# Stacked gate features and 64-column gate products in a cross-attention layer on Trainium2

## The reference

```python
emb = box_relational_embedding(boxes)      # [b, n, m, 16]: sin and cos of
                                           # 100 * log-distance (x, y) and 100 * log-size (w, h)
g = relu(einsum('bnmd,hd->bhnm', emb, Wg) + bg)
a = einsum('bhqd,bhkd->bhqk', q, k) / sqrt(64)
mn = softmax(log(clip(g, 1e-6)) + a, axis=-1)
out = einsum('bhqk,bhkd->bqhd', mn, v) @ Wo.T + bo
```

## Time and profile before

| | |
|---|---|
| Time, three runs | 1159.33, 1161.57, 1162.9 us; median 1161.57 us |
| The profiled execution | 1160.38 us, with a span of 1158.5 us |
| Mean granted clock of TensorE | 0.925 of full speed |
| PE, DVE, ACT, POOL busy | 83%, 71%, 59%, 62% of the span |
| First attention | from the start to about 476 us |
| Period of one box in its steady part | 23.7 us |

### The profile page before, as it was taken

One profiled execution on the slowest core, in us unless ns is written; L12 is line 12 of the kernel. 1 busy time (PEld: TensorE's weight loads), 2 busy tenths in 40 slices (PEclk: granted clock), 3 DMA queues, 4 the chain that ended last, 5 costly groups with the idle time before them and its releaser, 6 DMA issues.

```text
span 1158.5 us, 32871 instructions
## 1 busy us (share of the span) xinstructions
PE 958.8 (83%) x12178; PEld 778.2 (67%) x12178; DVE 822.9 (71%) x1947; ACT 683.9 (59%) x1338; POOL 712.6 (62%) x811
## 2 busy tenths in 40 slices
PE   0549999999999974679878469993899999999996
PEld 0346777777777753445554358871799999999995
DVE  3988887788778867468777689966566566666663
ACT  2457888888888863065426368864354444444452
POOL 2988888876776672034512569974566666666672
PEclk9878999999999997589989679985899999999998
DMA  9276776787677755500001000002553225832251
GB/s 285 66 197 138 137 143 157 161 194 151 153 155 143 135 121 137 187 7 1 1 26 44 5 2 21 21 21 92 170 156 94 32 45 166 259 88 32 31 143 14
DMA packets 52117, 119.65 MB, mean 103 GB/s; under 512 B 7616, under 2 KB 30144, under 8 KB 51632
## 3 DMA queue, kind: packets, MB, share of 16 engines
q0 software_dynamic: 14144, 35.48, 21.3%
q1 hardware_dynamic: 35520, 80.71, 20.5%
q10 hardware_dynamic: 2352, 2.10, 0.6%
HBM read 212.54 MB, written 37.85 MB: 216 GB/s over the span
## 4 chain that ended last, share of the span: by engine, by line
PE 51%; DVE 17%; POOL 11%; ACT 9%; issue 6%; DMA 4%; ACTq 0%; SPq 0%; POOLq 0%; DVEq 0%
PE bank L2107 17%; PE bank L2121 9%; POOL PT L560 5%; PE bank L1786 5%; PE bank L1689 3%; ACT EX L1393 2%; PE bank L1728 2%; PE bank L1766 2%; DVE h L1063 2%; DVE nmx L1177 2%; PE bank L1937 2%; ACT L1362 1%; PE bank L1721 1%; PE bank L1899 1%; ACT fks L1362 1%
## 5 line engine op out<-in xcount | busy, mean ns | idle before, releaser
L1623 ACT ACTIVATE yg<-bank,bms 128x128 f32<-128x128 f32 x312 | 105.7, 363 | 113.1 <-PE bank L2107 106.0
L1296 DVE TENSOR_TENSOR hm<-hf,hm 128x256 f16<-128x256 f32 x156 | 66.8, 428 | 99.7 <-ACT hm L1630 94.2
L2107 PE MATMUL bank<-xT,wm_even 128*128 128x128 f16 x1920 | 117.7, 221 | 3.1 <-DVE hf L1291 1.8
L1291 DVE SCALAR_TENSOR_TENSOR hf<-bank,bms,yg 128x128 f32<-128x128 f32 x312 | 98.6, 346 | 26.9 <-ACT yg L1623 25.8
L707 POOL DMA_INDIRECT out_x<-ys,sidx x39 | 62.7, 1608 | 86.2 <-DVE ys L1310 86.2
L2107 PEld LDWEIGHTS bank<-xT,wm_even 128*128 128x128 f16 x1920 | 111.5, 99 | 6.2 <-DVE hf L1291 3.9
L2107 PE MATMUL bank<-xT,wm_odd 128*128 128x128 f16 x1824 | 110.1, 219 | 2.3 <-DVE hf L1291 2.3
L2107 PEld LDWEIGHTS bank<-xT,wm_odd 128*128 128x128 f16 x1824 | 104.2, 98 | 4.9 <-DVE hf L1291 2.4
L1630 ACT ACTIVATE hm<-hf 128x256 f16<-128x256 f32 x156 | 64.6, 414 | 69.0 <-DVE hf L1291 68.2
L560 POOL TENSOR_TENSOR PT<-PT 128x512 f16<-128x512 f32 x64 | 72.3, 1158 | 42.7 <-ACT PT L1419 42.7
L619 POOL TENSOR_TENSOR h<-h 128x512 f16<-128x512 f32 x32 | 40.6, 1281 | 81.8 <-DVE h L1063 79.8
(11 more groups left out here) (308 smaller groups left out, 2658.7 us busy)
## 6 DMA issues: line engine op xcount, KB each, us to landing
wm_even<-expert_weights SPq DMA_DIRECT2D x60, 1024.0 KB
wm_odd<-expert_weights SPq DMA_DIRECT2D x57, 1024.0 KB
expert_weights<-in_wcat POOLq DMA_DIRECT2D x16, 768.0 KB, 8.0
wsp<-expert_weights SPq DMA_DIRECT2D x16, 768.0 KB, 4.3
wsp<-in_wcat POOLq DMA_DIRECT2D x16, 768.0 KB, 10.8
expert_weights<-wsp SPq DMA_DIRECT2D x16, 768.0 KB, 3.3
Lst<-gate_tables SPq DMA_DIRECT2D x48, 68.0 KB, 5.9
gate_tables<-Lw SPq DMA_DIRECT2D x6, 512.0 KB, 4.6
```

Of the source, the lines that this page charges most:

```text
L1291: v.scalar_tensor_tensor(hf[:, (c // 2) % 2, c % 2, :], bank[c % 4][:, MT:2 * MT], bms[:, par, FC + c:FC + c + 1], yg[:, c % 4, :], ALU.ad ...
L1296: v.tensor_tensor(hm16[:, par, 1, c - 1:c + 1, :], hf[:, q % 2, :, :], hm16[:, par, 0, c - 1:c + 1, :], ALU.subtract).then_inc(m_hl, 1)
L1623: s.activation(yg[:, c % 4, :], bank[c % 4][:, 0:MT], ACT.Gelu, bias=bms[:, par, c:c + 1]).then_inc(m_g, 1)
L2107: ins = t.matmul(bank[c % 4][:, w * MT:(w + 1) * MT], wm16[par][:, wp, col:col + P], xT16[:, par, xp * KD + kk, :], start=(n == 0), stop=( ...
```

## The change

The feature tile is laid out anew: its rows are now four groups (q) of 32, each with 4 queries times 8 features. For each box, transfers on the chip build `Fst`, 96 rows by 4 groups by 1024 columns: rows 0 to 31 and 32 to 63 hold the high part of group q, rows 64 to 95 its low part. The weights become a tile of 96 rows by 64 columns (16 heads x 4 queries): high, low, high. One product over 96 rows then sums all three pairs, and a gate of two j takes eight products of 64 columns (two j times four q) where it took six of 256. The result goes to the same bank, in steps of 4 out of 16 columns.

`F16s` now has one buffer and so has `Fst`. New on SP are `stack_high(b)`, 8 transfers of 64 KB, behind `s_fhi` and the gates of box b-1, and `stack_low(b)`, 4 transfers of 64 KB, behind `s_flo`. They stand: `stack_high(0)` ahead of `store_tables(0)`, `stack_low(0)` behind the first table loads; those of box b-1 in the place of box b, behind `load_tables(b)` and ahead of `store_half` and `load_half`; those of box 15 ahead of the last but one `store_half`. PE's gate 0, ACT's fp16 copy and POOL's `feature_low` wait for all stacks of their box or of the box before. The loads of box coordinates are now two of 1 MB (four of 512 KB before), and `We` is smaller. DVE's reciprocal (L882) counts on another semaphore.

```diff
+QN = 4
+QR = 2 * QN * 4
+FR = 3 * QR
+STK = 16 * 3 * (NN // QN)
-        F16s = sb("F16s", [P, 2, 2, NJ * N], F16, l0)
+        F16s = sb("F16s", [P, 2, NJ * N], F16, l0)
+        Fst = sb("Fst", [P, NN // QN, NJ * N], F16, l0)
...
+            def stack_high(b):
+
+                sp.wait_ge(s_fhi, b + 1)
+                if b:
+                    sp.wait_ge(s_gf, 4 * b)
+                for q in range(NN // QN):
+                    for k in range(2):
+                        sp.dma_start(Fst[k * QR:k * QR + QR, q, :], F16s[q * QR:q * QR + QR, 0, :]).then_inc(s_fst, 16)
+
+            def stack_low(b):
+
+                sp.wait_ge(s_flo, b + 1)
+                for q in range(NN // QN):
+                    sp.dma_start(Fst[2 * QR:3 * QR, q, :], F16s[q * QR:q * QR + QR, 1, :]).then_inc(s_fst, 16)
+
             for par in range(2):
                 next_ctx(par, par)
+            stack_high(0)
             store_tables(0)
             for par in range(2):
                 load_tables(par)
+            stack_low(0)
             for par in range(2):
                 load_half(0, par, True)
...
+            for b in range(2, B):
+                par = b % 2
+                if b < B - 2:
+                    next_ctx(b, par)
+                if b == NJ:
+                    store_tables(1)
+                load_tables(b)
+                stack_high(b - 1)
+                stack_low(b - 1)
+                store_half(b // 2 - 1, par)
+                load_half(b // 2, par)
+
+            stack_high(B - 1)
+            stack_low(B - 1)
             store_half(E - 1, 0)
             sp.wait_ge(s_qf, 6 * B)
...
             def feature_low(n, par):
                 gp.wait_ge(s_fhi, n + 1)
-                nc.gpsimd.tensor_tensor(F16s[:, par, 1, :], fs, F16s[:, par, 0, :], ALU.subtract).then_inc(s_flo, 1)
+                if n:
+                    gp.wait_ge(s_fst, STK * n)
+                nc.gpsimd.tensor_tensor(F16s[:, 1, :], fs, F16s[:, 0, :], ALU.subtract).then_inc(s_flo, 1)
...
-                if first > 1:
-                    ac.wait_ge(s_gf, 4 * n - 4)
-                s.activation(F16s[:, par, 0, :], fs, ACT.Copy).then_inc(s_fhi, 1)
+                if n:
+                    ac.wait_ge(s_fst, STK * n)
+                s.activation(F16s[:, 0, :], fs, ACT.Copy).then_inc(s_fhi, 1)
...
                 if g == 0:
-                    pe.wait_ge(s_flo, b + 1)
+                    pe.wait_ge(s_fst, STK * (b + 1))
...
-                    for n, (wp, fp) in enumerate(PAIRS):
-                        ins = t.matmul(bk[:, jj * 256:(jj + 1) * 256], F16s[:, par, fp, j * N:(j + 1) * N], We16[:, wp, :], start=False,
-                                       stop=(n == 2), skip_group_check=True)
+                    part = bk[:, jj * 256:(jj + 1) * 256].rearrange("p (h q i) -> p q h i", h=H, q=NN // QN)
+                    for q in range(NN // QN):
+                        ins = t.matmul(part[:, q, :, :], Fst[0:FR, q, j * N:(j + 1) * N], We16[0:FR, :], start=False, stop=True,
+                                       skip_group_check=True)
```

More of the change, by code:

```diff
@@ L122, in build @@
         R16 = sb("R16", [P, 2, 2, N], F16, l0)
-        We = sb("We", [P, H * NN], F32, l0)
-        We16 = sb("We16", [P, 2, H * NN], F16, l0)
+        We = sb("We", [P, H * QN], F32, l0)
+        We16 = sb("We16", [P, H * QN], F16, l0)
         WoT = sb("WoT", [P, CH, D], F32, l0)
@@ L339, in _ @@
             sp.dma_start(AB[:, :, :], a["AB"]).then_inc(s_cs, 16)
-            sp.dma_start(We[:, :], a["We"]).then_inc(s_cs, 16)
+            sp.dma_start(We[0:FR, :], a["We"]).then_inc(s_cs, 16)
             for j in range(3):
@@ L346, in _ @@
             sp.dma_start(boxn[:, :, :], a["boxn"]).then_inc(s_cw, 16)
-            for xy in range(2):
-                for e in range(2):
-                    sp.dma_start((cm, rows)[e][64 * xy:64 * xy + 64, :], a["boxm"][xy, e, :].partition_broadcast(64)).then_inc(s_cw, 16)
+            for e in range(2):
+                sp.dma_start((cm, rows)[e][:, :], a["boxm"][e]).then_inc(s_cw, 16)
             sp.dma_start(bqk[:, :, :], a["bqk"]).then_inc(s_o, 16)
@@ L881, in take_pv @@
                         dv.wait_ge(s_oe, 4 * c + f - 1)
-                    v.reciprocal(rden[:, f % 2, :].unsqueeze(2), ps[:, :, DK:DK + 1]).then_inc(s_rd, 1)
-                    dv.wait_ge(s_rd, 4 * c + f + 1)
+                    step(v.reciprocal(rden[:, f % 2, :].unsqueeze(2), ps[:, :, DK:DK + 1]))
                     if f == 0 and not first:
@@ L932, in _ @@
             xn_low(1, 1)
-            dv.wait_ge(s_cw, 16 * 5)
+            dv.wait_ge(s_cw, 16 * 3)
             step(v.tensor_tensor(cn[:, :], boxn[:, :, 0], boxn[:, :, 1], ALU.add))
@@ L2157, in arrange @@
     bn = lohi.transpose(4, 2, 0, 1, 3)
-    a["boxn"] = c(np.broadcast_to(bn[:, None], (2, 4, NN, B, NJ, 2)).reshape(P, B * NJ, 2))
-    a["boxm"] = c(boxes.reshape(T, 2, 2).transpose(2, 1, 0))
+    bn = bn.reshape(2, NN // QN, QN, B, NJ, 2).transpose(1, 0, 2, 3, 4, 5)
+    a["boxn"] = c(np.broadcast_to(bn[:, :, None], (NN // QN, 2, 4, QN, B, NJ, 2)).reshape(P, B * NJ, 2))
+    bm = boxes.reshape(T, 2, 2).transpose(1, 2, 0)
+    a["boxm"] = c(np.broadcast_to(bm[:, None, :, None], (2, NN // QN, 2, 4 * QN, T)).reshape(2, P, T))
     delta = np.array([(s >> 1) & 1 if s < 8 else 0 for s in range(SLOTS)])
@@ L2165, in arrange @@
     feat = lambda sc, dl, fr: Wg[:, sc * 8 + dl * 2 + fr]
-    We = np.zeros((2, 2, 2, NN, H, NN), np.float32)
+    We = np.zeros((3, 2, 2, 2, QN, H, QN), np.float32)
     for xy in range(2):
@@ L2169, in arrange @@
             for fr in range(2):
-                for nn in range(NN):
-                    We[xy, sc, fr, nn, :, nn] = feat(sc, xy, fr)
-    a["We"] = We.reshape(P, H * NN)
+                for i in range(QN):
+                    We[:, xy, sc, fr, i, :, i] = feat(sc, xy, fr)
+    a["We"] = We.reshape(FR, H * QN)
     AB = np.zeros((SLOTS, 2, H), np.float32)
@@ L2183, in arrange @@
     for p in range(P):
-        sc, fr = (p >> 5) & 1, (p >> 4) & 1
+        sc, fr = (p >> 3) & 1, (p >> 2) & 1
         cst[p, 0], cst[p, 1] = turn[fr], 0.25 * sc
```

9 lines of the change are left out of this document (5 added, 4 removed).

## The result

The changed kernel takes 1181.38 us (median of 4 runs, 1178.33 to 1182.59) beside 1160.45 for the kernel before: ratio 1.0176, 95% interval 1.0146 to 1.0206. It is slower, as predicted, but by 21 us and not by 8 to 9; the time lies above the range, which ended at 1179.0. The profiled execution took 1178.33 us with a span of 1176.5, 18.0 us more than before.

The account below looks back on a forecast made before the run. A 23.7 us chain of waits through ACT, POOL and PE, without the gate products, was taken as the bound; 0.8 + 2.4 + 5.0 = +8.2 us on 1160.38 gave 1168.6, plus 1.2 for the median: 1169.8 us, range 1164.0 to 1179.0.

Parts of the forecast that it names:

- What bounds the kernel: Steady box of the first attention: a 23.7 us chain of waits without the gate products bounds it, not PE's work.
- that sign of being right: Steady box: PE's idle time ahead of the value products at about 1.4 us, with the period still 23.7.
- Part 1: Gate products on PE: a gate falls from 1.08 to 0.68 us, a box by 1.6 us; term 0.
- Part 2: Stacks in a steady box: complete by 229.1 us at the median landing, gate 0 at 230.98; term 0.
- Late stacks in every box: Rival, slower: twelve stacks land 9.2 us after the last issue, delaying every gate 0; 1180 us, chance 0.10.
- Part 3: Box 7: its stacks, queued behind the second tables, delay gate 0; +2.4 us, bounds +1.0 and +7.2.
- Part 4: Feed-forward weights: box 15's stacks ahead of these loads on SP delay DVE; +5.0 us, bounds +4.2 and +8.1.
- Part 5: First box: stacks and tables fall among POOL's conversions, less a shorter gate; +0.8 us, bounds -0.5 and +2.5.
- gates on the path: Rival, faster: PE is the limit, so 1.6 us of each box come off; 1144 us, chance 0.06.
- cheap issues: Rival, no change: SP issues a small stack transfer in 0.05 us, not 0.42; 1164 us, chance 0.11.
- dear products: Rival, slower: a small gate product costs the same 127 ns as one of 256 columns; 1177 us, chance 0.04.
- the ring: 23.7 us chain per box: exponentials, ACT, POOL's low parts, PE's value products to scores, next exponentials; gate products outside it.

Follow-up runs that it names:

- b1: Kernel before the change, with one of three pairs of feature products in the gates (two products instead of six), no stacks; 1160.35 us, ratio 1.0013.
- b2: Changed kernel with 128 unused products on PE ahead of gate 0 of box 7, filling its wait; 1176.98 us, ratio 1.0183 to the kernel before.
- a2: Changed kernel with the high stack of box 0 issued behind the first table stores, ahead of the wait for their landing; 1176.84 us, ratio 1.0141.
- a3: Changed kernel with the low stack of box 15 issued behind the four feed-forward weight loads instead of ahead; 1177.18 us, ratio 1.0148.
- a1: Changed kernel with both stacks of box 7 issued ahead of the second set of tables; 1181.61 us, ratio 1.0184 to the kernel before.
- b3: Changed kernel with POOL's two converting transfers of expert weights held back until the first tables have landed; 1167.41 us, one run, no ratio.
- e1: Kernel before, early feed-forward loads, stacks moved in their best order and waited for ahead of gate 0 but never read; 1157.96 us, ratio 1.0046.
- e2: Same as e1 but PE does not wait for the stacks, which are moved and never read; 1155.90 us, ratio 1.0026 to the kernel before.
- c1: Changed kernel with box 7's stacks issued between the second set of table stores and SP's wait for their landing; 1171.48 us, ratio 1.0126.

## Why the prediction was right or wrong

**What bounds the kernel: right.** Neither the ordinary periods of after nor those of b1 moved, and the idle time grew where the prediction put it ahead of the second half of the scores (0.62 us for 0.6). The larger part appeared ahead of the row scores (1.39 us), where PE waits for DVE, and not ahead of the value products (0.25 us, as before, for a forecast 1.45): that sign of being right did not come.

**Part 1, gate products: right.** 43 ns for a forecast 45; a gate takes 0.65 us for 0.68. The Trainium skill ("TensorE: Matmul & The Clock Gate", section "LDWEIGHTS (loading the stationary operand)") gives 107 ns for each weight load by its formula; as a pitch of products with a load each, the trace of after disagrees as that of before did.

**Part 2, ordinary boxes: right, with margin.** Less the 4.0 us of the first box the low stack of after starts at 221.9, as predicted, and with a median landing of 2.0 us (in ordinary boxes at most 2.7) it is there 4 to 6 us before gate 0. The DMA share rose to 0.85 where 0.82 was predicted. Late stacks in every box did not occur.

**Part 3, box 7: the mechanism right, three sizes wrong.** With 4.0 us taken off, the table loads start at 248.5, as they did. From there: (1) "twelve issues at 0.42 us" took 7.76 us in place of 5.0. The price came from a table load of 16 rows, and a stack transfer of 32 rows takes 0.59 us and a gap of 0.04 (that the rows make the difference is not shown). The last issue starts 2.6 us later than I had it. (2) The landing was 5.35 us, not 3.5: +1.85. I chose the value near the local row, but POOL's conversion was already in flight, which I had named and priced at 1.3 us. (3) The clock was left out, although the first box showed a granted 0.50 behind a stretch without products: a wait of 7 us halves it, and b2 prices that at 2.8 us. With 2.4 predicted, 2.6 and 1.85 explain a lateness of 6.85 us, and b2, whose clock stays up, measures 6.6. With the half clock this is the 9.4 us seen. My upper bound of +7.2 had the longest landing but neither the issue price nor the clock. So the steps that failed are the price of an issue, the landing, and a clock term put at nothing without a reason. The last is also the least certain size: a2 and a3 have 1.7 and 4.0 us for it. The text also had both parts of the stack ready "long before" the table loads; a1 shows the low part only 2 to 3 us ahead of them, which is why a1's move failed.

**Part 4, feed-forward weights: right.** +4.65 for +5.0. The four low issues took 2.41 us in place of 1.7, and the last landing was 0.7 us shorter than before (8.80, 9.52). The lower bound of +4.2 has no working: the four issues alone gave +4.4. The 0.6 us that came back behind it was not foreseen.

**Part 5, the first box: wrong, +4.0 for +0.8.** The step that failed is the one that costs the push by volume ("0.26 MB ... at 2.9 us for 1 MB"). Volume did not matter. What mattered is that the eight issues of high stacks, 5.06 us, moved the tables behind POOL's conversions on the DMA engines, and that SP stands for the tables' landing. I had these stacks and the conversions in one sentence and did not follow the wait `s_ts` that lies between them; a2 and b3 each undo it in their own way. The 0.5 us that a shorter gate was to give back are not shown: the next period is 1.5 us shorter, but in e1 and e2, with the gates of before, as well.

**The sum.** The forecast was 1169.8 us and the measured time is 1181.4. Of this miss 9.8 us are the terms: 3.2 in the first box, 7.0 in box 7, and -0.4 in the rest. The other 1.9 us are that the median of after lies 3.1 us above its profiled execution where that of before, of three runs, lay 1.2. What they are is not shown: executions in which one more stack is late (e1) or in which the lower clock lasts longer (a3) would fit. Of the rivals, late stacks have come true in one place only; gates on the path, cheap issues and dear products are ruled out.

## What to carry to other kernels

Where one queue both issues and waits, price what a new transfer pushes behind the queue's next wait, and which other queue's long transfer it is now behind: here eight cheap issues made a landing 7 us longer and the first box 4.0 us later, and moving them a few lines gave 3.6 of these back. Small transfers belong in the time that the queue stands anyway. Check that the engine that a change relieves is in the ring at all; a kernel with part of its work left out tells that in one run.

## What the runs showed of the hardware that was not expected

- The issue of a 64 KB stack transfer, between two tiles in on-chip memory, takes SP 0.59 us and a gap of 0.04 in after, beside 0.42 with the gap for the table loads of 68 KB. It is not steady: eight took 4.97 us there, 5.89 in c1 and 6.94 in e1.
- The landing of the same transfer is 1.9 to 2.7 us for the low stacks of ordinary boxes, issued when no transfer of POOL is in flight. Beside a converting transfer of POOL it is 4.8 to 5.5 us in box 7 of after, 4.3 in e2 and up to 7.6 in e1. For the table stores after and b3 show both, 10.1 and 2.6 us, with one wait between them. The Trainium skill ("DMA: Bandwidth & Descriptors", section "Anatomy of one DMA — SWDGE (gpsimd) path") gives a fixed 2.0 us for transfers that POOL issues; the stacks are issued by SP, and their least landing, 1.9 us, agrees with it, while the landings beside other transfers are longer.
- A wait of 7.4 to 7.5 us on PE costs another 1.7 (a2), 2.8 (after) or 4.0 us (a3) at the lower clock, measured against b2, whose unused products fill the wait and keep the granted clock at 1.00.
